# Experts' first product with the tokens stationary and split weights, and scores as two row groups

## What is computed

```python
# layer 0's experts
logits = x @ router_w + router_b
max_prob, max_ind = jnp.max(softmax(logits)), jnp.argmax(...)
for e in range(8):
    a, g = jnp.split(x @ w1[e], 2, axis=1)      # w1[e]: 256 x 2048
    y = jax.nn.silu(a) * g @ w2[e]              # w2[e]: 1024 x 256
    out = jnp.where((max_ind == e)[:, None], y, out)
out = out * max_prob
# both attentions, per batch b and head h
scores = q @ k.T / sqrt(16)                     # 512 x 64 per batch and head
out = softmax(scores) @ v
```

## Time and profile before

| | |
|---|---|
| median of 3 runs | 629.05 us (628.01 to 654.66) |
| the profiled execution | 628.45 us |
| its span, first to last instruction | 626.6 us |
| busy: TensorE, VectorE, ScalarE, GpSimd | 520.7, 383.9, 258.9, 260.4 us |
| granted TensorE clock over the span | 0.912 of full |

### The profile page before, as it was taken

The page is one execution under the profiler, slowest core; times in us unless marked ns, Lnnn a source line. Parts: engine busy times, 40 slices in busy tenths (PEclk is TensorE's granted clock), DMA queues, the critical chain, the costliest instruction groups (busy, mean ns, idle before and its releaser), DMA issues.

```text
span 626.6 us, 10395 instructions
## 1 busy us (share of the span) xinstructions
PE 520.7 (83%) x3422; PEld 390.8 (62%) x3430; DVE 383.9 (61%) x782; ACT 258.9 (41%) x441; POOL 260.4 (42%) x321
## 2 busy tenths in 40 slices
PE   5966989899694489999999999939588898567994
PEld 2433755658484289999999999934244454334653
DVE  4278888788824754343334422215788998858993
ACT  1133746354470053343334432311344444435984
POOL 3553435253410282211111111038245867737996
PEclk9976999989896579999999999985799999787999
DMA  6930010000146225751564201013000000000101
GB/s 207 292 118 1 1 34 2 33 2 1 35 157 214 71 64 187 248 207 45 206 234 156 95 17 33 14 45 97 4 1 0 2 0 1 1 1 0 35 33 67
DMA packets 28631, 46.36 MB, mean 74 GB/s; under 512 B 2381, under 2 KB 24921, under 8 KB 26553
## 3 DMA queue, kind: packets, MB, share of 16 engines
q1 hardware_dynamic: 24328, 39.02, 18.5%
q0 software_dynamic: 1680, 4.59, 2.5%
q10 hardware_dynamic: 2592, 2.36, 1.1%
HBM read 38.36 MB, written 7.60 MB: 73 GB/s over the span
## 4 chain that ended last, share of the span: by engine, by line
PE 47%; DVE 31%; issue 7%; POOL 6%; ACT 4%; DMA 3%; DVEq 0%; SPq 0%; ACTq 0%; POOLq 0%
PE bank L908 18%; PE bank L920 7%; DVE s_max L1350 5%; DVE probs L1358 4%; DVE p_sum L1368 4%; PE bank L656 4%; PE bank L769 3%; PE bank L986 2%; DVE ew L1309 2%; PE bank L667 2%; DVE stats L1287 2%; ACT probs L1053 2%; DVE xn L1309 2%; DVE x_res L1497 1%; DMA ew<-in_L_ffn_w 1%
## 5 line engine op out<-in xcount | busy, mean ns | idle before, releaser
L908 PE MATMUL bank<-q_t,ew 128*128 128x128 f32 x1152 | 137.5, 278 | 1.1 <-DVE probs_t L1626 0.5
L908 PEld LDWEIGHTS bank<-q_t,ew 128*128 128x128 f32 x1152 | 133.6, 194 | 2.7 <-DVE probs_t L1626 1.7
L464 POOL TENSOR_TENSOR probs<-probs,p_rcp 128x1024 f32<-128x1024 f32 x32 | 60.9, 1906 | 115.0 <-DVE p_rcp L1371 115.0
L1626 DVE TENSOR_TENSOR probs_t<-bank,probs 128x512 f32<-128x512 f32 x36 | 24.8, 690 | 75.5 <-ACT probs L1175 75.5
L667 PE MATMUL bank<-k_bd,q_t 128*128 128x512 f32 x128 | 65.2, 628 | 3.5 <-ACT q_t L1048 3.5
L523 POOL TENSOR_TENSOR token_now<-token_of,carried 128x1 uint32<-128x1 uint32 x17 | 8.4, 491 | 124.3 <-PE bank L894 124.3
L681 PE MATMUL bank<-ident,probs 128*128 128x128 f32 x256 | 38.4, 299 | 23.7 <-POOL probs L464 22.7
L681 PEld LDWEIGHTS bank<-ident,probs 128*128 128x128 f32 x256 | 31.8, 153 | 41.6 <-POOL probs L464 30.7
L1053 ACT ACTIVATE probs<-probs 128x1024 f32<-128x1024 f32 x32 | 33.9, 1058 | 57.5 <-DVE probs L1358 57.5
L1083 ACT COPY probs_t<-bank 128x512 f32<-128x512 f32 x64 | 34.7, 589 | 47.1 <-PE bank L681 47.0
L1350 DVE TENSOR_REDUCE s_max<-bank 128x8 f32<-128x512 f32 x64 | 40.3, 671 | 21.4 <-PE bank L667 21.3
(11 more groups left out here) (206 smaller groups left out, 1098.7 us busy)
## 6 DMA issues: line engine op xcount, KB each, us to landing
ew<-in_L_ffn_w SPq DMA_DIRECT2D x8, 2048.0 KB
ew<-in_L_ffn_w SPq DMA_DIRECT2D x8, 1024.0 KB, 5.8
slots_y<-xn ACTq DMA_DIRECT2D x18, 128.0 KB, 1.9
x_res<-in_x SPq DMA_DIRECT2D x4, 512.0 KB, 6.9
token_rows<-ew SPq DMA_DIRECT2D x4, 512.0 KB, 3.2
out_rows<-x_res SPq DMA_DIRECT2D x3, 512.0 KB, 2.9
w<-in_L_xattn_W SPq DMA_DIRECT2D x2, 512.0 KB, 8.7
ew<-in_L_ffn_w_gate SPq DMA_DIRECT2D x1, 1024.0 KB, 8.7
```

What stands on the lines that cost most here:

```text
L464: nc.gpsimd.tensor_tensor(p, p, p_rcp[:, i, :].unsqueeze(2).to_broadcast([P, H, M]), ALU.mult).then_inc(s["p_norm"], 1)
L908: last = nc.tensor.matmul(o[:, P * j:P * j + P], ew1[:, s, k, c0:c0 + P], xs_t[:, par, k, :], start=(k == 0), stop=(k == DK - 1))
```

## The change

Four edits, and what follows from them.

- First product of the experts: the turned rows are split into `xs_hi` and `xs_lo` and stand; the weights, split into `ew1_hi` and `ew1_lo`, move 512 columns at a time. A half `q` has two parts (gate and up), a part six fp32r matmuls. `ew1_hi` lies over memory that is free by then, `ew1_lo` overwrites `ew1`.
- Units then come out with the tokens on the partitions, so TensorE turns them (`turn_units`), and cast and subtraction read the turned units from PSUM.
- The split of the first weights: for expert 0 on ScalarE and GpSimd ahead of the routing's end, for the others on ScalarE and VectorE in four pieces spread over `between_tiles`, which is the body of `next_expert` now.
- Scores: `k_bd` holds two row groups of 64, so a half's eight heads take 256 columns; a tile has four products of 64 rows and 256 columns, group 0 to one PSUM bank and group 1 to the other.

```diff
+        ew1_hi01 = under("ew1_hi01", w2, [P, 2 * FE], -DK * F1 * 4)
+        ew1_hi10 = sb("ew1_hi10", [P, 2 * FE], F32R)
...
-        k_bd = sb("k_bd", [P, DK, B, HC * M])
...
+        k_bd = sb("k_bd", [P, DK, B, GH * M])
...
+        xs_hi = under("xs_hi", q_t, [P, 2, DK, P])
+        xs_lo = under("xs_lo", q_t, [P, 2, DK, P], N * 4)
...
+        ew1_hi00 = under("ew1_hi00", probs, [P, 2 * FE])
...
+        ew1_lo = under("ew1_lo", ew1, [P, 2, DK, 2 * FE])
...
-        xs_t = q_t[:, 0, :].rearrange("p (s k t) -> p s k t", s=2, k=DK)
...
-        act_t = probs_t
+        sil = probs_t[:, 0].rearrange("p j t -> p (j t)").rearrange("p (q f) -> p q f", q=2)
+        act = probs_t[:, 1].rearrange("p j t -> p (j t)").rearrange("p (q f) -> p q f", q=2)
...
-        def next_expert(engine, t, prepare):
...
                 with engine.If(e < E - 1):
                     with engine.If(e % 2 == 0):
-                        prepare(e + 1, 1)
+                        body(e + 1, 1)
                     with engine.Else():
-                        prepare(e + 1, 0)
+                        body(e + 1, 0)
+                with engine.Else():
+                    body(None, None)
+            with engine.Else():
+                body(None, None)
...
+        def w1_part(w, s, p):
+
+            c0 = FE * (p % 2) + 512 * (p // 2)
+            if w is ew1_hi:
+                return [ew1_hi[s][k][:, c0:c0 + 512] for k in range(DK)]
+            return [w[:, s, k, c0:c0 + 512] for k in range(DK)]
...
-                            k_bd[:, m, b, :].rearrange("p (h s) -> p h s", h=HC),
-                            k_t[:, m, b * M:b * M + M].unsqueeze(1).to_broadcast([P, HC, M]),
-                            head_mask[:].unsqueeze(2).to_broadcast([P, HC, M]), ALU.mult).then_inc(p_kbd, 1)
+                            k_bd[:, m, b, :].rearrange("p (h s) -> p h s", h=GH),
+                            k_t[:, m, b * M:b * M + M].unsqueeze(1).to_broadcast([P, GH, M]),
+                            group_mask[:].unsqueeze(2).to_broadcast([P, GH, M]), ALU.mult).then_inc(p_kbd, 1)
...
+            for p in range(4):
+                pool.wait_ge(a_w1, p + 1)
+                for lo, w, hi in zip(w1_part(ew1_lo, 0, p), w1_part(ew1, 0, p), w1_part(ew1_hi, 0, p)):
+                    last = nc.gpsimd.tensor_tensor(lo, w, hi.bitcast(F32), ALU.subtract)
+                last.then_inc(lo_w1, 1)
...
-                    last = nc.tensor.matmul(s_bank[i % 2][m][:], q_t[:, m, P * i:P * i + P],
-                                            flat(k_bd[:, m, bass.ds(n, 1), :]), start=True, stop=True)
+                    for g in range(G):
+                        rows = slice(GP * g, GP * g + GP)
+                        last = nc.tensor.matmul(s_bank[i % 2][g][:, GH * M * m:GH * M * m + GH * M],
+                                                q_t[rows, m, P * i:P * i + P], flat(k_bd[rows, m, bass.ds(n, 1), :]),
+                                                start=True, stop=True)
...
-                for o, base in ((a_bank[q], 0), (g_bank[q], FE)):
-                    for j in range(4):
-                        c0 = base + (4 * q + j) * P
-                        for k in range(DK):
-                            last = nc.tensor.matmul(o[:, P * j:P * j + P], ew1[:, s, k, c0:c0 + P],
-                                                    xs_t[:, par, k, :], start=(k == 0), stop=(k == DK - 1))
-                last.then_inc(m_up, 1)
+                for half, o in enumerate((a_bank[q], g_bank[q])):
+                    part = 2 * q + half
+                    pe.wait_ge(lo_w1, 4 * e + part + 1)
+                    hi, lo = w1_part(ew1_hi, s, part), w1_part(ew1_lo, s, part)
+                    for k in range(DK):
+                        x_hi, x_lo = xs_hi[:, par, k, :], xs_lo[:, par, k, :]
+                        for n, (x, w) in enumerate(((x_hi, hi[k]), (x_hi, lo[k]), (x_lo, hi[k]))):
+                            last = nc.tensor.matmul(o[:], x, w, start=(k == 0 and n == 0),
+                                                    stop=(k == DK - 1 and n == 2))
+                    last.then_inc(m_up, 1)
...
+            def turn_units(t, q, first_tile):
+
+                pe.wait_ge(m_act, 2 * t + q + 1)
+                if not first_tile:
+                    pe.wait_ge(m_lo, 2 * t - 1 + q)
+                for j in range(4):
+                    last = nc.tensor.transpose(u_bank[q][:, P * j:P * j + P], act[:, q, P * j:P * j + P], ident[:])
+                last.then_inc(m_at, 1)
...
+                expand(t, par, e, s, 0, first_tile)
                 if not first_tile:
                     contract(t - 1, 1 - par, expert(t - 1) % 2, 1)
+                turn_units(t, 0, first_tile)
                 rows_in(t + 1, 1 - par, n + 1 if par else n)
-                expand(t, par, s, loads, 1, first_tile)
-                pe.wait_ge(v_w2, e + 1)
+                expand(t, par, e, s, 1, first_tile)
+                pe.wait_ge(v_w2, 2 * e + 2)
                 if not first_pair:
                     pe.wait_ge(m_y, t - 1)
                 contract(t, par, s, 0)
+                turn_units(t, 1, first_tile)
...
+            act.wait_ge(m_w1[0], 16)
+            for p in range(4):
+                for hi, w in zip(w1_part(ew1_hi, 0, p), w1_part(ew1, 0, p)):
+                    last = nc.scalar.copy(hi, w)
+                last.then_inc(a_w1, 1)
+            act.wait_ge(m_w2[0], 16)
+            for q in range(2):
+                nc.scalar.copy(w2_part(ew2_hi, 0, q), w2_part(ew2, 0, q)).then_inc(a_w2, 1)
...
+            def upper_units(t, q):
+                act.wait_ge(m_at, 2 * t + q + 1)
+                nc.scalar.copy(flat(act_hi[:, 4 * q:4 * q + 4, :]), bank[4 + q][:]).then_inc(m_hi, 1)
...
+            def upper_first(e, s, p):
+                if p == 0:
+                    act.wait_ge(m_w1[s], 16 * (e // 2 + 1))
+                for hi, w in zip(w1_part(ew1_hi, s, p), w1_part(ew1, s, p)):
+                    last = nc.scalar.copy(hi, w)
+                last.then_inc(a_w1, 1)
...
+            def between_tiles(t, par, stored, e, s):
+
+                if e is not None:
+                    upper_first(e, s, 0)
+                    upper_first(e, s, 1)
+                upper_units(t, 1)
+                expert_gate(t + 1, 0, False)
+                if e is not None:
+                    upper_first(e, s, 2)
+                    upper_first(e, s, 3)
+                if stored is not None:
+                    act.wait_ge(m_st[0], 16 * stored)
+                    act.wait_ge(m_st[1], 16 * stored)
+                expert_out(t, par)
+                upper_units(t + 1, 0)
+                expert_rows(t + 2, par)
+                if e is not None:
+                    upper_second(e, s, 0)
+                expert_gate(t + 1, 1, False)
+                if e is not None:
+                    upper_second(e, s, 1)
 
...
+            def lower_first(e, s, p):
+                dve.wait_ge(a_w1, 4 * e + p + 1)
+                for lo, w, hi in zip(w1_part(ew1_lo, s, p), w1_part(ew1, s, p), w1_part(ew1_hi, s, p)):
+                    last = nc.vector.tensor_tensor(lo, w, hi.bitcast(F32), ALU.subtract)
+                last.then_inc(lo_w1, 1)
...
+            def expert_units(t, q, first_tile):
+                dve.wait_ge(m_sil, 2 * t + q + 1)
+                dve.wait_ge(m_up, 4 * t + 2 * q + 2)
+                if not first_tile:
+                    dve.wait_ge(m_at, 2 * t + q - 1)
+                nc.vector.tensor_tensor(act[:, q, :], bank[2 + q][:], sil[:, q, :], ALU.mult).then_inc(m_act, 1)
...
+            def lower_units(t, q):
+                dve.wait_ge(m_hi, 2 * t + q + 1)
+                nc.vector.tensor_tensor(flat(act_lo[:, 4 * q:4 * q + 4, :]), bank[4 + q][:],
+                                        flat(act_hi[:, 4 * q:4 * q + 4, :]).bitcast(F32), ALU.subtract).then_inc(m_lo, 1)
...
+            def between_tiles(t, par, e, s):
+
+                if e is not None:
+                    lower_first(e, s, 0)
+                    lower_first(e, s, 1)
+                lower_units(t, 1)
+                expert_units(t + 1, 0, False)
+                if e is not None:
+                    lower_first(e, s, 2)
+                    lower_first(e, s, 3)
+                lower_units(t + 1, 0)
+                expert_rows(t + 2, par)
+                if e is not None:
+                    lower_second(e, s, 0)
+                expert_units(t + 1, 1, False)
+                if e is not None:
+                    lower_second(e, s, 1)
 
             pairs = slot_pairs(dve)
```

168 lines of the change are left out of this document (80 added, 88 removed).

## The result

The changed kernel takes 642.73 us (median of 4 executions, 640.84 to 648.32); the kernel before, run beside it, 628.53 (627.75 to 654.66). The ratio is 1.0252, with a 95% interval of 1.0218 to 1.0286: slower. (The 654.66 is one execution over 4% above the other three of its kernel; such slow ones do not count in the ratios.) The forecast was 622, range 612 to 634.

A forecast was written before the change was run, and what follows sets the result against it. It took TensorE to bound the expert stage, with scores and short VectorE routing operations on the chain elsewhere. Experts -7.6, routing +6.0 and scores -5.2 gave -6.8 on 628.45, 621.65; with the median 0.6 higher, 622 us, range 612 to 634.

The forecast's parts named there:

- Step 1: TensorE in an expert tile: 9.67 us a tile with the split first product, a gain of 0.7 us a tile.
- 0.13 for the branch: Expert tile on TensorE: the branch adds 0.13 us to the 9.67 us tile.
- the walk of step 2: Timeline of a new-expert tile from its first product's end: turn done at 1.86 us, next tile's first half until 4.65.
- the sign that the prediction had named for itself: Experts: the forecast is wrong if ordinary tiles take over 10 us.
- Step 2: VectorE and ScalarE in expert tiles: waits of 5.9 us at one-tile experts, stage 185.3 us for 192.9, term -7.6 us.
- 0.2 late: New experts with two tiles or more: VectorE has the lower units at 4.85 us, TensorE wants them at 4.65.
- Step 3: Routing ahead of the experts: GpSimd's eight subtractions of expert 0's first weights delay VectorE's routing operations, term +6.0 us.
- the price of 3.7 us: Routing: the delay if every VectorE SBUF operation gets in between two of GpSimd's subtractions, about 3.7 us.
- the upper bound, 7.1: Routing: the delay if the scans ahead of the routing operations wait for GpSimd too, 7.1 us.
- Step 4: Scores as two row groups side by side: 0.7 us saved a tile, only calls on the chain counting, term -5.2 us.
- rival B: Scores: the row groups don't overlap, time 628.2 us; chance 0.14.
- Rival C: Seven tiles with new weights: casts and subtractions not hidden, 42 us at full exposure for 5.9 counted, 658 us; chance 0.12.

The follow-up runs named there:

- turn_behind: The changed kernel with the second turn of a tile's units issued at the head of the next tile, behind TensorE's branch: 635.3 us, ratio 1.0128.
- copy_subs: turn_behind with VectorE's subtractions of the split expert weights replaced by plain copies (expert 0's first weights excepted): 628.2 us, ratio 0.9995.
- scores_only: The kernel before with only the scores, spread keys and VectorE's two operations on them as changed: 625.0 us, ratio 0.9963.
- bias_early: scores_only with GpSimd's output-bias addition in layer 0 issued one place earlier, ahead of the fourth tile's normalisation: 623.3 us, ratio 0.9944.

## Why the prediction was wrong, point by point

**Step 1, an expert tile.** The durations were right: 0.230 us from matmul to matmul (0.233 said), turns 0.44 for four, no price for the waits for lo_w1. The tile is 9.47 us where nothing disturbs it and 9.74 in the mean of turn_behind less its waits, for 9.67 said. What failed is the term "0.13 for the branch". It was read from the kernel before, where the branch lies under twelve matmuls, and carried over to an order in which it lies under four turns and a wait. The step asked what a late lo_w1 would cost, and never what stands behind the new wait of the second turn on TensorE. In the walk of step 2 too, TensorE goes from the turn (to 1.86) straight into the next tile's first half. There is 2.2 us of register work between two pairs of tiles and 1.3 to 1.7 within a pair, of which 0.3 to 1.5 show in thirteen tiles: 11.6 us, and 11.2 in turn_behind's difference. This one omission is half of the miss, which is 22.6 us by the ratio (15.8 measured, -6.8 said), and no rival held it. The ordinary tile at 10.9 us is the sign that the prediction had named for itself (over 10 us).

**Step 2, VectorE and ScalarE.** The waits at the one-tile experts were said to be 5.9 us and are 6.4 (5.9 in turn_behind: 2.08, 1.66 and 2.20). The "0.2 late" in the longer experts is 1.07 to 1.32 us, three times, once the pause on TensorE no longer hides it: VectorE's register work was taken as 1.05 us and is 1.81. With that (3.4 us), 1.35 us of one half of the second product at a low clock, 1.1 us for the mean tile and 1.2 us at the last tile, turn_behind's stage is 192.1 us. The forecast's 185.3, which counts to the last output, is 184.9 to the last matmul. Even with two fifths of VectorE's weight work gone the stage is 185.9 us (copy_subs), 6.4 below the kernel before and not 7.6.

**Step 3, the routing.** Right in kind and nearly in size: +6.0 said, +6.7 measured, and 0.4 more for the rows' lower part (L1707), which now stands ahead of the first product and was left out. The way was another. It was to be one long VectorE operation; it is many short ones that wait for one of GpSimd's at a time. GpSimd's eight took 9.99 us, not 8.03, and two scans go through between two of them. The Trainium skill (SBUF — State Buffer, "SBUF: two separate sides") has this as a lock held for one instruction at a time. The trace agrees with that here, and the price of 3.7 us that the prediction drew from that rule was too low because more operations are held than it counted. The row that it took instead, L1619 waiting for all eight of GpSimd's, was not to be relied on: in scores_only the same operation came in between two of them (2.69 us). GpSimd began where it was said to, 2.05 us behind l_max. But the scans, which the forecast let pass, are held too: it is nearly the case of the upper bound, 7.1. So that +6.0 came so close is in part luck.

**Step 4, the scores.** The row groups do overlap: rival B is out. The gain on TensorE is 0.85 us a tile (1.98 to 1.13) where 0.7 was said. What failed is the step from the chain to the time: "only the calls on the chain count: 5 x 0.7, and 1.7 of the cold 3.67". The calls were on the chain, and a second chain was as long within 0.1 us. scores_only and bias_early show it for layer 0: GpSimd's addition and VectorE's x_n. For layer 1 it was not looked into. The change of the scores alone gains 2.3 us by the ratio, not 5.2. By the traces it gains 1.4 in layer 0's scores and 1.7 in layer 1's, and 2.0 in the expert stage, which the step did not count; the profiled execution gives 1.4 back in the tail, whose time goes in steps.

**Rival C** gave the right side for a reason that was not the main one. Its mechanism, casts and subtractions that are not hidden, is worth 9.5 us in turn_behind's expert stage (6.1 for weights, 3.4 for the lower units behind them), of 42 at full exposure. That is 3.6 more than the forecast counted, and alone would have left the kernel within 2%.

**The sum.** Said: -7.6 + 6.0 - 5.2 = -6.8. Measured by stretches: +11.0 for the experts, +7.2 from l_max to the first product and -5.7 for the other three, +12.4. Those three are the least sure: the start to the first scores alone varies from 23.9 to 27.1 us among the kernels with the changed scores. By the ratio the difference is 15.8 us (0.0252 x 628.5). With scores_only's -2.3 in place of the -5.7 the sum is 15.9; that it fits so well is luck, as the 2.3 may be 0.2 to 4.5. Against the forecast the pause costs 11.2 us, the rest of the expert stage 7.4, the routing 1.2 and the scores about 2.9.

The Trainium skill (Perfetto Trace Analysis, "Sequencer Loop") says that a sequencer pushes an engine's instruction into a queue, where it waits for its semaphores, and carries out control instructions itself. From that one might take it that a branch runs past an instruction that waits. The listing above says otherwise for this place: the branch ran at 315.66 us, 0.06 after the multiplication that the turn waits for had ended, and so it is at 15 of 17 boundaries.
